# A later panel's product moved into the last steps of a two-stage graph kernel, and four PSUM banks for the later panels

## The reference

```python
S   = (adj + adj.T) * 0.5
M   = S + eye(2048)
deg = sum(M, axis=1)
d   = where(deg > 0, deg ** -0.5, 0)
y   = (adj @ (d[:, None] * M * d[None, :])) @ x
out = layernorm(x + y)        # over the 512 columns, eps 1e-5
```

## Time and profile before

| | us |
|---|---|
| median of 3 runs | 429.55 (429.06 to 430.82) |
| the profiled execution | 428.08 |
| its span, first to last instruction | 426.3 |
| PE busy | 393.6 (92%) |
| DVE busy | 241.3 (57%) |
| ACT busy | 111.6 (26%) |
| POOL busy | 74.0 (17%) |
| DMA queue, share of 16 engines | 49.8% |

### The profile page before, as it was taken

The page is one execution under the profiler, slowest core; times in us unless marked ns, Lnnn a source line. Parts: engine busy times, 40 slices in busy tenths (PEclk is TensorE's granted clock), DMA queues, the critical chain, the costliest instruction groups (busy, mean ns, idle before and its releaser), DMA issues.

```text
span 426.3 us, 5406 instructions
## 1 busy us (share of the span) xinstructions
PE 393.6 (92%) x1822; PEld 325.6 (76%) x1822; DVE 241.3 (57%) x463; ACT 111.6 (26%) x195; POOL 74.0 (17%) x109
## 2 busy tenths in 40 slices
PE   3479999997799699999999999999999999999994
PEld 3467788885588488888888888888888888888883
DVE  0656777773704402222266227777777777777752
ACT  1124444432603402222222222222222222222210
POOL 3466878752000000000000000000000000000000
PEclk9659999999999999999999999999999999999999
DMA  8999855430004736226232256565555555655500
GB/s 241 303 315 288 243 165 185 136 100 2 0 2 98 174 74 148 49 51 147 50 100 50 49 127 152 137 151 138 146 137 149 139 146 137 150 138 151 122 25 25
DMA packets 73969, 54.76 MB, mean 128 GB/s; under 512 B 3552, under 2 KB 62048, under 8 KB 73952
## 3 DMA queue, kind: packets, MB, share of 16 engines
q1 hardware_dynamic: 73952, 54.54, 49.8%
HBM read 41.94 MB, written 4.19 MB: 108 GB/s over the span
## 4 chain that ended last, share of the span: by engine, by line
issue 73%; PE 14%; DVE 7%; DMA 2%; SPq 2%; POOL 1%; ACT 0%; POOLq 0%; DVEq 0%
PE ps L412 3%; PE ps L391 3%; PE ps L393 3%; PE ps L392 3%; DVE lots_r L674 2%; DMA lots_s<-adj 2%; PE ps L420 1%; DVE u_lo L686 1%; POOL rstd L382 1%; DVE lots_s L633 1%; DVE store L633 1%; DVE deg L648 0%; SPq L284 0%; PE ps L435 0%; SPq L274 0%
## 5 line engine op out<-in xcount | busy, mean ns | idle before, releaser
L393 PE MATMUL ps<-z,w_lo 128*128 128x512 f32 x256 | 99.7, 389 | 0.0
L391 PE MATMUL ps<-z,w_hi 128*128 128x512 f32 x256 | 99.7, 389 | 0.0
L392 PE MATMUL ps<-z,w_hi 128*128 128x512 f32 x256 | 99.7, 389 | 0.0
L391 PE MATMUL ps<-u_hi,w_hi 128*128 128x512 f32 x176 | 69.4, 394 | 4.1 <-DVE z_raw L700 4.1
L616 ACT ACTIVATE w_hi<-turned 128x512 fp32r<-128x512 f32 x64 | 39.8, 632 | 122.9 <-DVE turned L741 122.9
L393 PE MATMUL ps<-u_hi,store_lo 128*128 128x512 f32 x176 | 69.3, 394 | 0.0
L392 PE MATMUL ps<-u_lo,w_hi 128*128 128x512 f32 x176 | 69.1, 392 | 0.0
L741 DVE STREAM_TRANSPOSE turned<-strips 128x512 f32<-128x512 f32 x64 | 65.5, 1069 | 0.0
L382 POOL TENSOR_TENSOR rstd<-var_eps,mhalf 128x1 f32<-128x1 f32 x16 | 8.8, 548 | 303.6 <-DVE var_eps L791 303.6
L700 DVE SCALAR_TENSOR_TENSOR z_raw<-ps,dinv_half,z_raw 128x512 fp32r<-128x512 f32 x16 | 11.9, 750 | 86.4 <-ACT z_raw L572 86.4
L391 PEld LDWEIGHTS ps<-z,w_hi 128*128 128x128 f32 x256 | 48.1, 188 | 10.0
(11 more groups left out here) (78 smaller groups left out, 432.7 us busy)
## 6 DMA issues: line engine op xcount, KB each, us to landing
strips<-adj SPq DMA_DIRECT2D x64, 256.0 KB, 4.5
z<-z_raw SPq DMA_DIRECT2D x64, 128.0 KB, 2.4
u_x<-x SPq DMA_DIRECT2D x16, 256.0 KB, 4.7
x_res<-x SPq DMA_DIRECT2D x16, 256.0 KB, 2.6
out<-y_out SPq DMA_DIRECT2D x16, 256.0 KB, 2.1
lots_s<-adj SPq DMA_DIRECT2D x13, 256.0 KB, 4.6
store<-adj SPq DMA_DIRECT2D x2, 512.0 KB, 5.7
col_slot<-adj SPq DMA_DIRECT2D x1, 896.0 KB, 9.8
```

The source lines that it names most:

```text
L391: nc.tensor.matmul(out_, hi, mov_hi, start=first, stop=False)
L392: nc.tensor.matmul(out_, hi, mov_lo, start=False, stop=False)
L393: return nc.tensor.matmul(out_, lo, mov_hi, start=False, stop=last)
```

## The change

Five things are changed together.

1. `multiply_rest(0, ...)` (panel 3) starts in step 13: four of its 16 blocks at the end of each of the steps 13, 14 and 15, two after the product of step 14, two after that of step 15. Before, 14 blocks came after the product of step 14. Its high and low parts are made in steps 8 to 11, one chunk of four blocks a step, behind lot_high on ACT and behind u_low on DVE.
2. The sum of panel 3 stays in bank `tp[1]`, which now ends its work as mirror bank in step 12. `mirror_corner` uses `tp[0]` and waits for the chunk of the next step to be added; `transpose_cols` from step 14 on waits for corner_low.
3. The later panels go round four banks, `acc_rest[n % 4]`, with other waits on PE.
4. The two extra lots hold steps 0 and 1 alone, and the steps from 2 on go round the four kept ones. SP waits for the product of step k-4 from k = 6 on.
5. On ACT `u_high` comes ahead of `corner_high`.

```diff
@@ -129,8 +129,8 @@
         csum = ps[:, G + 1]
         tp = [ps[:, n].rearrange("p (b c) -> p b c", c=P) for n in (G + 2, G + 3)]
         parked = [ps[:, m].rearrange("p (b c) -> p b c", c=P) for m in range(G)]
-        acc_rest = [ps[:, G + 3], csum]
-        acc2 = [ps[:, 0], ps[:, 1]]
+        acc_rest = [ps[:, G + 3], csum, ps[:, G + 2], ps[:, 0]]
+        acc2 = [ps[:, 1], ps[:, 2]]
         s_const = sem("constants_made")
         s_ident = sem("ident_made")
@@ -189,8 +189,11 @@
+        def slot_of(k):
+            return KEPT + k if k < SLOTS - KEPT else k % KEPT
         def lot(k, lots, part):
-            j = k % SLOTS
+            j = slot_of(k)
             return lots[0][:, j, part] if j < KEPT else lots[1][:, j - KEPT, part]
         def lot_sum(k):
@@ -283,7 +286,7 @@
                         sp.wait_ge(s_tc, chunk_at(k - 2))
                     sp.dma_start(col(k, k + 1, NB), a_cols[k, :, k + 1:NB]).then_inc(s_in[k], 16)
                 if k >= SLOTS:
-                    sp.wait_ge(s_prod, k - SLOTS + 1)
+                    sp.wait_ge(s_prod, k - KEPT + 1)
                 b = max(k, NR)
                 sp.dma_start(lot_sum(k)[:, b - NR:G], a_rows[k, :, b:NB]).then_inc(s_in[k], 16)
                 sp.dma_start(u_x[:, k], x_rows[k]).then_inc(s_x[k], 16)
@@ -407,6 +410,8 @@
             def transpose_cols(k, i, b0, b1):
                 pe.wait_ge(s_add, chunk_at(k) + i)
+                if k > NR + 1:
+                    pe.wait_ge(s_mlo, k - 1 - NR)
                 for b in range(b0, b1):
                     src = row(k, b, b + 1) if b == k else col(k, b, b + 1)
                     last = nc.tensor.transpose(tp[0][:, b - b0], src[:, 0], ident[:])
@@ -422,11 +427,9 @@
             def mirror_corner(k):
                 pe.wait_ge(s_diagl, k - NR + 1)
-                pe.wait_ge(s_mir, MIRRORS)
-                if k > NR:
-                    pe.wait_ge(s_mlo, k - NR)
+                pe.wait_ge(s_add, chunk_at(k + 2))
                 for b in range(k + 1, NB):
-                    last = nc.tensor.transpose(tp[1][:, b - k - 1], row(k, b, b + 1)[:, 0], ident[:])
+                    last = nc.tensor.transpose(tp[0][:, b - k - 1], row(k, b, b + 1)[:, 0], ident[:])
                 last.then_inc(s_tm, 1)
             def col_sums(k):
@@ -454,9 +457,11 @@
             def multiply_rest(n, tiles):
                 p = REST[n]
                 for t in tiles:
+                    if n == 0 and t == 0:
+                        pe.wait_ge(s_mir, MIRRORS)
                     if t % CB == 0:
                         pe.wait_ge(s_lo, NC * n + t // CB + 1)
-                    last = passes(acc_rest[n % 2], hi_of(n)[:, t], store_lo[:, p - 1, t], u_hi[:, t], u_lo[:, t],
+                    last = passes(acc_rest[n % 4], hi_of(n)[:, t], store_lo[:, p - 1, t], u_hi[:, t], u_lo[:, t],
                                   t == 0, t == NB - 1)
                 if t == NB - 1:
                     last.then_inc(s_mm, 1)
@@ -482,16 +487,19 @@
                         col_sums(k)
                         summed = True
                 if k > NR:
+                    multiply_rest(0, range(CB * (k - NR - 1), CB * (k - NR)))
                     mirror_corner(k - 1)
             for m in range(G + 1):
                 multiply_unit(NB - 2, m)
-            multiply_rest(0, range(NB - 2))
+            multiply_rest(0, range(CB * (NB - NR - 1), NB - 2))
             for m in range(G + 1):
                 multiply_unit(NB - 1, m)
             multiply_rest(0, range(NB - 2, NB))
             for n in range(1, len(REST)):
-                if n >= 2:
-                    pe.wait_ge(s_zl, G + n)
+                if n == 2:
+                    pe.wait_ge(s_mlo, G - 1)
+                elif n > 2:
+                    pe.wait_ge(s_zl, n + 2 if n > 3 else 1)
                 multiply_rest(n, range(NB))
             def multiply2(q, j, ready=lambda i: None):
@@ -533,9 +541,9 @@
             def corner_high(k):
                 act.wait_ge(s_tm, MIRRORS + k - NR + 1)
-                act.wait_ge(s_prod, NB - SLOTS)
-                j = (k + 1) % SLOTS
-                nc.scalar.activation(lots_r[0][:, j:j + NB - 1 - k, 1, k - NR], tp[1][:, 0:NB - 1 - k],
+                act.wait_ge(s_prod, NB - KEPT)
+                j = slot_of(k + 1)
+                nc.scalar.activation(lots_r[0][:, j:j + NB - 1 - k, 1, k - NR], tp[0][:, 0:NB - 1 - k],
                                      ACT.Copy).then_inc(s_mhi, 1)
             def first_high(n):
@@ -552,15 +560,15 @@
             def rest_high(n, cs=range(NC)):
                 if n == 0:
-                    act.wait_ge(s_prod, NR)
+                    act.wait_ge(s_prod, SLOTS - KEPT)
                 elif n == 1:
                     act.wait_ge(s_tc, chunk_at(NB))
                 elif n == 2:
                     act.wait_ge(s_prod, NB)
                 else:
                     act.wait_ge(s_mm, n - 1 if n > 3 else 1)
-                act.wait_ge(s_mir, MIRRORS)
-                act.wait_ge(s_diag, NR - 1)
+                act.wait_ge(s_mir, mirror_at(REST[0] + 1) if n == 0 else MIRRORS)
+                act.wait_ge(s_diag, REST[0] if n == 0 else NR - 1)
                 for c in cs:
                     nc.scalar.activation(hi_of(n)[:, CB * c:CB * c + CB], store[:, REST[n] - 1, CB * c:CB * c + CB],
                                          ACT.Copy).then_inc(s_hi, 1)
@@ -573,22 +581,20 @@
             def z_rest(n):
                 act.wait_ge(s_mm, n + 1)
-                z_high(G + 1 + n, acc_rest[n % 2])
+                z_high(G + 1 + n, acc_rest[n % 4])
             for k in range(NB):
                 if 1 <= k - 1 < NR:
                     store_mirrors(k - 1)
-                elif k > NR:
-                    corner_high(k - 1)
                 if k >= 1:
                     u_high(k - 1)
+                if k > NR:
+                    corner_high(k - 1)
                 lot_high(k)
                 if k < len(FIRST):
                     first_high(k)
-                if k == NB - 2:
-                    rest_high(0, range(2))
-                if k == NB - 1:
-                    rest_high(0, range(2, NC))
+                if NR - NC <= k < NR:
+                    rest_high(0, range(k - NR + NC, k - NR + NC + 1))
             u_high(NB - 1)
             rest_high(1)
             act.wait_ge(s_prod, NB)
@@ -676,9 +682,9 @@
             def corner_low(k):
                 dve.wait_ge(s_mhi, k - NR + 1)
-                j = (k + 1) % SLOTS
+                j = slot_of(k + 1)
                 slots = slice(j, j + NB - 1 - k)
-                nc.vector.tensor_tensor(lots_r[0][:, slots, 0, k - NR], tp[1][:, 0:NB - 1 - k],
+                nc.vector.tensor_tensor(lots_r[0][:, slots, 0, k - NR], tp[0][:, 0:NB - 1 - k],
                                         lots_r[0][:, slots, 1, k - NR], ALU.subtract).then_inc(s_mlo, 1)
             def u_low(k):
@@ -687,7 +693,8 @@
                                                ALU.mult, ALU.subtract).then_inc(s_ul, 1)
             def rest_low(n, cs=range(NC)):
-                dve.wait_ge(s_cb, main_parts(NB))
+                dve.wait_ge(s_cb, main_parts(REST[0] if n == 0 else NB))
+                dve.wait_ge(s_near, REST[0] if n == 0 else NB - 1)
                 for c in cs:
                     dve.wait_ge(s_hi, NC * n + c + 1)
                     tiles = slice(CB * c, CB * c + CB)
@@ -719,10 +726,9 @@
                     u_low(k - 1)
                     if k - 1 < len(FIRST):
                         first_low(k - 1)
-                if k == NB - 2:
-                    rest_low(0, range(2))
+                if NR - NC <= k < NR:
+                    rest_low(0, range(k - NR + NC, k - NR + NC + 1))
             lot_low(NB - 1)
-            rest_low(0, range(2, NC))
             u_low(NB - 1)
             nc.vector.tensor_scalar(dinv_half[:], dinv[:], 0.5, None, ALU.mult).then_inc(s_dhalf, 1)
             rest_low(1)
@@ -734,7 +740,7 @@
             z_low(4, acc_first)
             def z_rest(n):
-                z_low(G + 1 + n, acc_rest[n % 2])
+                z_low(G + 1 + n, acc_rest[n % 4])
             def turn(q, i, j):
                 g = GROUPS[i]
```

## The result

The changed kernel takes 424.74 us in the median of 4 runs (422.57 to 425.17), the kernel before 430.19 us beside it: ratio 0.9876, 95% interval 0.9837 to 0.9915. It is faster, by 5.45 us between the medians. The forecast was 423.8 us with a range of 421.8 to 427.3 us. In a later set of runs the same kernel had 424.06 us against 430.43 us, ratio 0.9861 (0.9835 to 0.9886). One execution of the kernel before in that later set took 808.14 us, and the ratio leaves it out as slow.

A forecast was written before the change was run, and what follows sets the result against it. PE was taken as the bound, with idle time before n = 2 and in the first stage's last steps. Profiled 428.08 - 6.0 + 0 + 0.3 + 0 = 422.4 us, or 423.8 us as median; range 421.8 to 427.3 us.

The forecast's parts named there:

- Panel n = 2 and its bank: Third later panel, at 146.61 us: a third bank removes PE's wait on z_raw and the clock fall, 6.0 us gained.
- What was feared to come late: Later panels n = 3 and n = 4: their operands or banks might be late; judged in time, n = 3 with 4 us left.
- Panel 3 in steps 13 to 15: Last steps of the first stage: twelve matmuls ahead of mirror_corner delay its chain by their own length, so 0 gained.
- The sign that was named: Steps 13 to 15: three PE waits on u_lo of about 2.2, 2.0 and 1.8 us remain, 2.7 us further apart.
- The parts of panel 3: Steps 8 to 11: a new DVE subtraction of 0.69 us each delays the next add, together 0.3 us lost.
- the first rival: Steps 9 to 12: DVE and POOL block each other, costing 2.4 us in place of 0.3, 425.9 us; chance 0.12.
- The lots: Lot loads on four places: landing in about 3 us within a step of at least 4.93 us, step 11; cost 0.
- The clock: PE's granted clock: 1.00 from 116 us to the second stage.
- From the profile to the median: Whole kernel: the profiled execution stands 1.5 us below the median; the same difference turns 422.4 us into 423.8 us.

The follow-up runs named there:

- the exchange of the two lines: Changed kernel with mirror_corner put ahead of the four blocks of panel 3 in steps 13, 14 and 15: 416.35 us, ratio 0.9681.
- the early corner: Kernel before with mirror_corner of step k-1 behind the first unit of step k's product, not the last; nothing of the change: 421.55 us, ratio 0.9801.
- the parts one step later: Changed kernel with the four chunks of panel 3's high and low parts made in steps 9 to 12: 423.7 us, ratio 0.9883.

## Why the prediction was right, point by point

*Panel n = 2 and its bank, -6.0 us.* Right in place and size. The four banks alone moved the median by 6.3 us, and in the trace of the change n = 2 follows without a wait. What was feared to come late did not: PE is busy throughout from 142 to 300 us.

*Panel 3 in steps 13 to 15, 0.* Right. The kernel without the banks has ratio 0.999, and from mirror_corner to the next product it is 2.93 us as ever. The reason given, that the chain begins with mirror_corner and the blocks stand ahead of it, is shown by the exchange of the two lines. The sign that was named, waits on u_lo of 2.2, 2.0 and 1.8 us, came in pieces: 1.26 and 0.76, 1.02 and 0.74, 1.69 us.

*The parts of panel 3, +0.3 us.* The sum was close, 0.53 us in the trace, but the working was wrong. I had counted 0 for step 9, 0.2 us for step 10 and 0.1 us for step 11; it was all in step 9, and less than 0.05 us in each of the others. For step 10 I had put the whole 0.69 us of the new instruction against a slack of 0.46 us; but from u_low to the add it is 1.26 us in the change (80.94 to 82.20 us) and was 0.85 us before, so the add came only 0.41 us later. In step 9 I had looked only at DVE's idle time and not at when ACT would have the high part ready. It was 0.34 us late, and that let POOL in front: the mechanism of the first rival, in one of four places. The reason given against it, that POOL's long additions come later in a step, was wrong there: one of 0.73 us began at 75.88 us, in the very place. That the sum came out near is luck in part. The later chunks had the mechanism too, but with the roles exchanged (POOL waited, 0.92 us for 0.45 us), and POOL had time.

*The lots, 0.* Right: landing in 3.2 to 3.9 us for the lots of steps 6 to 13, where 3 us was expected and 4.9 us were to be had. The shortest of these steps, though, was not step 11 with 4.93 us but step 12 with 4.53 us (90.24 to 94.77 us before, 91.33 to 95.87 us in the change). The lot issued at its start, that of step 13, landed in 3.3 us.

*The clock.* This was the wrong one. I had said 1.00 from 116 us on, since the profiled execution before showed no fall behind the same holes. By its time and mean clock it was one of few without. The profiled execution of the change had a fall there and lost 1.5 us; with 0.5 us of a longer load phase this is why the two profiled executions differ by 3.4 us only (428.08 to 424.71 us), the medians by 5.45 us.

*From the profile to the median.* The 1.5 us between the profiled execution and the median were carried over as a constant. In the change the profiled execution took 424.71 us beside a median of 424.74 us. That the offset was the missing fall of the clock fits the numbers (mean clock 0.974 in that execution, 0.969 or 0.970 in most), but no trace was taken of an execution of the kernel before with such a fall. The profiled execution was forecast at 422.4 us, 2.3 us too low, and the median 0.9 us too low. That the second is closer is luck in part: the 1.5 us were added without knowing what they were, and they were of the size of the fall that the forecast had at nothing.

The accounts of the two profiled executions, in us: -6.0 hole and clock before n = 2; +0.5 step 9; +1.5 clock behind the second hole; +0.5 in the start and the load phase (step 3 begins at 35.15 us before and 35.70 us after, with the same instructions up to there, and at 34.50 us in the second profile of the change). Together -3.5 of -3.4.

## What to carry to other kernels

Work that is to fill a wait must stand behind the instruction that starts the waited-for chain; ahead of it the work delays the chain by its own length and gains nothing. Find the first instruction of the chain, and see how early it can be issued: here an earlier place alone closed three holes. And split a change into its parts before it is kept: here one of five parts had all the gain.

## What the runs showed of the hardware

The granted clock can fall behind holes of about 2 us, but does so in some executions and not in others with holes equal to 0.01 us; behind the 4 us hole it fell in all four traces that had one (the kernel before, the one without the banks, the lots alone, the early corner: clock 0.83, 0.83, 0.83 and 0.85 from 142 to 152 us). Of the seven traces with the 2 us holes it fell in three, all of them among the four of the changed order (the change, the one without the banks, the parts one step later); the three of the old order show none (the kernel before, the four banks alone, the lots alone). Whether the order matters can't be told from so few. A fall behind the 2 us holes cost 1.5 us each time (38.26 to 38.27 us from step 13 to n = 1, against 36.74 us). Behind the 4 us hole it cost 1.8 us in three traces and 3.0 us in the one without the banks, where matmuls took 0.63 us up to 155 us (279.7 and 281.0 us from the start of n = 2 to the end, against 277.9 us). How the chip decides isn't shown by these runs.

The mean clock of an execution is a rough sign only. It was 0.969 or 0.970 mostly in the kernel before, 0.977 to 0.980 at best with one sort of hole removed, and 0.976 to 0.980 in all executions with both removed, whose times spread by 1.4 and 1.7 us (2.5 to 3.7 us in the kernel before). But it also holds the load phase, where the clock was 0.57 or 0.58 from 15 to 35 us in some traces and 0.66 in others, and the last 5 us, where PE is idle and it was 0.66 to 0.91. The trace of the parts one step later had the fall and a mean of 0.979; the one with the corner ahead had no hole there and 0.976.

A DVE subtraction with both inputs in SBUF and a POOL addition hold each other up, and the one that comes second pays: 0.94 us for 0.68 us on DVE, or 0.92 us for 0.45 us on POOL, while the first keeps its own time. The second ended 0.55 us (DVE) and 0.33 us (POOL) after the end of the first, so four fifths and three quarters of its own length (0.68 and 0.45 us) came behind it. That one of the two gets a shared pair of ports for its whole instruction is what the Trainium skill says in "SBUF — State Buffer", section "SBUF: two separate sides", and the trace agrees with it on both sides.
